# The last 32 rows of each expert, handled in two groups of four experts

## What is computed

```
mask1 = one_hot(argmax(softmax(tokens @ gate_w + gate_b)), 8)
pos   = number of earlier tokens of the same expert;  keep = pos < 160
dispatch = einsum('nec,nd->ecd', mask1 x one_hot(pos) x keep, tokens)
h          = gelu(dispatch @ w1 + b1)        # 8 experts, 160 x 256 -> 160 x 1024
expert_out = h @ w2 + b2                     # 160 x 1024 -> 160 x 256
out = x + gate probability x expert_out, put back at the token's row
```

## Time and profile before

| | us |
|---|---|
| median of three runs (1109.96 to 1110.98) | 1110.84 |
| the profiled execution's own time | 1106.06 |
| its span in the profile | 1104.1 |
| expert stage, first transpose to the last matmul of L778 | 1013.1 to 1094.1 |
| from there to the end of the span | 10.0 |

### The profile page before, as it was taken

The page is one execution under the profiler, slowest core; times in us unless marked ns, Lnnn a source line. Parts: engine busy times, 40 slices in busy tenths (PEclk is TensorE's granted clock), DMA queues, the critical chain, the costliest instruction groups (busy, mean ns, idle before and its releaser), DMA issues.

```text
span 1104.1 us, 40835 instructions
## 1 busy us (share of the span) xinstructions
PE 1066.6 (97%) x16195; PEld 869.6 (79%) x16195; DVE 882.3 (80%) x2652; ACT 796.4 (72%) x2319; POOL 244.1 (22%) x521
## 2 busy tenths in 40 slices
PE   6899999999999999999999999999999999988996
PEld 5678787787888788887787888788888778766996
DVE  6788798898888888888898888888888888874211
ACT  5778687788787787787787787787787787742221
POOL 1011212222222222212222222222222222221112
PEclk9999999999999999999999999999999999999998
DMA  7333422222221222112222221222212221001673
GB/s 202 109 101 102 154 63 67 68 68 64 60 64 44 61 62 57 49 50 60 61 61 61 60 60 42 59 56 56 48 48 58 58 61 36 17 12 47 207 249 110
DMA packets 69260, 82.04 MB, mean 74 GB/s; under 512 B 14331, under 2 KB 48076, under 8 KB 69072
## 3 DMA queue, kind: packets, MB, share of 16 engines
q1 hardware_dynamic: 64896, 75.06, 23.6%
q0 software_dynamic: 3360, 3.72, 1.0%
q10 hardware_dynamic: 816, 0.66, 0.2%
HBM read 64.79 MB, written 16.56 MB: 74 GB/s over the span
## 4 chain that ended last, share of the span: by engine, by line
PE 72%; DVE 18%; issue 4%; DMA 2%; ACT 1%; SPq 1%; POOL 1%; POOLq 0%; DVEq 0%; ACTq 0%
PE kps L416 12%; PE vps L428 12%; PE score L462 9%; PE score L448 5%; PE gather L477 5%; PE shared L486 5%; PE shared L501 4%; DVE prob L1092 4%; DVE nmx L1081 4%; PE score L778 3%; PE score L764 3%; PE shared L527 3%; DVE ctx_p L1073 2%; PE shared L405 2%; DVE th L1175 2%
## 5 line engine op out<-in xcount | busy, mean ns | idle before, releaser
L830 ACT ACTIVATE prob<-score,nmx 128x257 f32<-128x257 f32 x512 | 235.8, 475 | 95.8 <-DVE nmx L1081 95.8
L416 PE MATMUL kps<-ctx_p,wk_p 128*128 128x512 f32 x768 | 217.4, 411 | 0.0
L428 PE MATMUL vps<-wv_p,ctx_p 128*128 128x256 f32 x1536 | 215.5, 290 | 0.0
L1081 DVE TENSOR_REDUCE nmx<-score 128x2 f32<-128x514 f32 x256 | 165.2, 687 | 59.2 <-PE score L448 59.0
L428 PEld LDWEIGHTS vps<-wv_p,ctx_p 128*128 128x128 f32 x1536 | 191.7, 190 | 14.1 <-issue 12.7
L416 PEld LDWEIGHTS kps<-ctx_p,wk_p 128*128 128x128 f32 x768 | 138.1, 190 | 38.5 <-issue 13.6
L1092 DVE TENSOR_SCALAR prob<-prob,rsum 128x256 f32<-128x256 f32 x512 | 159.3, 354 | 9.1
L462 PE MATMUL score<-const,prob 128*128 128x128 f32 x1024 | 153.5, 278 | 5.5 <-DVE prob L1092 3.3
L1558 POOL TENSOR_TENSOR rstd<-ve,const 128x1 f32<-128x1 f32 x64 | 53.2, 831 | 464.6 <-DVE ve L1210 235.7
L462 PEld LDWEIGHTS score<-const,prob 128*128 128x128 f32 x1024 | 114.7, 141 | 16.3 <-DVE prob L1092 14.9
L847 ACT ACTIVATE ctx_p<-ctxT,nlast 128x256 fp32r<-128x256 f32 x256 | 116.0, 511 | 4.2 <-issue 4.2
(11 more groups left out here) (227 smaller groups left out, 1734.7 us busy)
## 6 DMA issues: line engine op xcount, KB each, us to landing
ctxT<-in_ctxT SPq DMA_DIRECT2D x128, 257.0 KB, 3.2
w<-in_w SPq DMA_DIRECT2D x16, 1024.0 KB, 8.1
xq<-in_x SPq DMA_DIRECT2D x32, 128.0 KB, 2.1
xr<-in_x SPq DMA_DIRECT2D x32, 128.0 KB
qbd<-qkT SPq DMA_DIRECT2D x248, 16.0 KB, 1.8
out<-row SPq DMA_DIRECT2D x31, 128.0 KB
slots<-row SPq DMA_DIRECT2D x10, 257.0 KB, 5.1
x_a<-slots SPq DMA_DIRECT2D x8, 129.0 KB, 2.1
```

Of the source, the lines that this page charges most:

```text
L416: last = mm(kps[:, :], wk_p[:, x, n, c * P:(c + 1) * P], ctx_p[:, y, n, 2 * r:2 * r + 2, :].rearrange("p j s -> p (j s)"), start=(n, x) == ...
L428: last = mm(vps[:, c, :], ctx_p[:, x, n, j, c * P:(c + 1) * P], wv_p[:, y, n, :], start=(n, x) == (0, LO), stop=(n, y) == (C - 1, LO))
L830: last = af(prob[:, m, :], score[:, m, 0:S], ACT.Exp, bias=nmx[:, m:m + 1], scale=1.0, accum_out=esum[:, m:m + 1])
L1081: v.tensor_reduce(nmx[:, 2 * c:2 * c + 2], score[:, 2 * c:2 * c + 2, 0:S], AX.X, ALU.max, negate=True).then_inc(s["max_done"], 1)
```

## The change

The 128-row part stays as it was. The 32-row parts of experts 0 to 3 share one tile of 128 partitions, and those of experts 4 to 7 another: they are loaded with four DMAs into 32 partitions each, transposed together, and copied with two instructions to the columns 128 to 159 of a `disp` that now has a place for every expert. The second bias is added in two instructions for the 128 columns and two for the 32 columns, the latter into `eo_rest`, which collects four experts; after experts 3 and 7 that tile is transposed, added (`fb`, 128 rows) and written with one indirect DMA. Loads of the first group are issued half by SyncE and half by ScalarE. The declarations of the new semaphores and unchanged lines are left out here.

```diff
--- before.py
+++ after.py
@@ -25,6 +25,7 @@
 CR = CAP - P
+GROUP = P // CR
 ROW = 2 * D + 2
@@ -167,14 +168,15 @@
-        y_a, y_b = sb("y_a", [P, 2, D]), sb("y_b", [CR, 2, D])
-        x_a, x_b = sb("x_a", [P, 2, ROW - D]), sb("x_b", [CR, 2, ROW - D])
+        y_a, y_b = sb("y_a", [P, 2, D]), sb("y_b", [P, 2, D])
+        x_a, x_b = sb("x_a", [P, 2, ROW - D]), sb("x_b", [P, 2, ROW - D])
         gelu_table = sb("gelu_table", [P, 1])
         table = sb("table", [P, 2])
-        disp = sb("disp", [P, C, CAP])
+        disp = sb("disp", [P, E, C, CAP])
         hid = sb("hid", [P, FT, CAP])
-        eo = sb("eo", [P, C, CAP])
-        fa, fb = sb("fa", [P, 2, D]), sb("fb", [CR, 2, D])
+        eo, eo_rest = sb("eo", [P, C, P]), sb("eo_rest", [P, C, P])
+        fa, fb = sb("fa", [P, 2, D]), sb("fb", [P, 2, D])
@@ -348,20 +351,28 @@
-            def load_rows(e, r, a_, b_, columns, done):
-                sp.dma_start(a_[:, r, :], slots[bass.ds(CAP * e, P), columns]).then_inc(s[f"{done}{r}"], 16)
-                sp.dma_start(b_[:, r, :], slots[bass.ds(CAP * e + P, CR), columns]).then_inc(s[f"{done}{r}"], 16)
+            def load_rows(e, r, dst, columns, done):
+                sp.dma_start(dst[:, r, :], slots[bass.ds(CAP * e, P), columns]).then_inc(s[f"{done}{r}"], 16)
+            def load_rest(g, dst, columns, done, members=range(GROUP)):
+                for m in members:
+                    e = GROUP * g + m
+                    sp.dma_start(dst[CR * m:CR * (m + 1), g, :], slots[CAP * e + P:CAP * (e + 1), columns]).then_inc(s[f"{done}{g}"], 16)
+            load_rows(0, 0, y_a, slice(0, D), "y_in")
+            load_rest(0, y_b, slice(0, D), "y_rest", range(1, GROUP, 2))
+            load_rows(1, 1, y_a, slice(0, D), "y_in")
             for r in range(2):
-                load_rows(r, r, y_a, y_b, slice(0, D), "y_in")
-            for r in range(2):
-                load_rows(r, r, x_a, x_b, slice(D, ROW), "x_in")
+                load_rows(r, r, x_a, slice(D, ROW), "x_in")
+            load_rest(1, y_b, slice(0, D), "y_rest")
+            for g in range(2):
+                load_rest(g, x_b, slice(D, ROW), "x_rest")
             for i in range(0, E // 2 - 1):
 ...
                     sp.wait_ge(s["dt_ps"], e + 1)
-                    load_rows(e + 2, r, y_a, y_b, slice(0, D), "y_in")
+                    load_rows(e + 2, r, y_a, slice(0, D), "y_in")
@@ -372,10 +383,11 @@
-                    sp.wait_ge(s[f"fin_out{r}"], 32 * i + 32)
-                    load_rows(e + 2, r, x_a, x_b, slice(D, ROW), "x_in")
+                    sp.wait_ge(s[f"fin_out{r}"], 16 * i + 16)
+                    load_rows(e + 2, r, x_a, slice(D, ROW), "x_in")
             for r in range(2):
-                sp.wait_ge(s[f"fin_out{r}"], 32 * (E // 2))
+                sp.wait_ge(s[f"fin_out{r}"], 16 * (E // 2))
+            sp.wait_ge(s["rest_out"], 32)
             sp.wait_ge(s["x2_out"], 16 * T)
@@ -725,20 +737,25 @@
             hps = [score[:, m, 0:3 * CAP].rearrange("p (f n) -> p f n", f=3) for m in range(3)]
-            dps = shared[:, 0:C * CAP].rearrange("p (c n) -> p c n", c=C)
+            dps, rps = sh_c, gather[:, :, 0, :]
             ops_ = score[:, 3, 0:C * CAP].rearrange("p (c n) -> p c n", c=C)
 ...
                 e = 2 * i + r
-                pe.wait_ge(s[f"y_in{r}"], 32 * (i + 1))
+                pe.wait_ge(s[f"y_in{r}"], 16 * (i + 1))
                 pe.wait_ge(s["dt_evac"], e)
                 for c in range(C):
-                    nc.tensor.transpose(dps[:, c, 0:P], y_a[:, r, c * P:(c + 1) * P], k["ident"])
-                    last = nc.tensor.transpose(dps[:, c, P:CAP], y_b[:, r, c * P:(c + 1) * P],
-                                               k["ident"][0:CR, 0:CR])
+                    last = nc.tensor.transpose(dps[:, c], y_a[:, r, c * P:(c + 1) * P], k["ident"])
                 last.then_inc(s["dt_ps"], 1)
+            def transpose_rest(g):
+                pe.wait_ge(s[f"y_rest{g}"], 16 * GROUP)
+                for c in range(C):
+                    last = nc.tensor.transpose(rps[:, c], y_b[:, g, c * P:(c + 1) * P], k["ident"])
+                last.then_inc(s["rest_ps"], 1)
@@ -747,21 +764,26 @@
                 for c in range(C):
-                    nc.tensor.transpose(kps[:, c * P:(c + 1) * P], eo[:, c, 0:P], k["ident"])
-                    last = nc.tensor.transpose(vps[0:CR, 0, c * P:(c + 1) * P], eo[:, c, P:CAP], k["ident"])
+                    last = nc.tensor.transpose(kps[:, c * P:(c + 1) * P], eo[:, c, :], k["ident"])
                 last.then_inc(s["et_ps"], 1)
+                if e % GROUP == GROUP - 1:
+                    pe.wait_ge(s["eo_rest"], e + 1)
+                    for c in range(C):
+                        last = nc.tensor.transpose(vps[:, 0, c * P:(c + 1) * P], eo_rest[:, c, :], k["ident"])
+                    last.then_inc(s["et_rest"], 1)
 ...
                 pe.wait_ge(s["dt_evac"], e + 1)
+                pe.wait_ge(s["rest_done"], e // GROUP + 1)
                 pe.wait_ge(s[f"w1_in{r}"], 16 * (i + 1))
 ...
                     for c in range(C):
-                        last = mm(hps[f // 3][:, f % 3, :], w1[:, r, c, f * P:(f + 1) * P], disp[:, c, :],
+                        last = mm(hps[f // 3][:, f % 3, :], w1[:, r, c, f * P:(f + 1) * P], disp[:, e, c, :],
                                   start=c == 0, stop=c == C - 1)
@@ -769,8 +791,10 @@
                     transpose_dispatched(i + (r + 1) // 2, (r + 1) % 2)
+                if once(e, 1):
+                    transpose_rest(1)
                 pe.wait_ge(s[f"w2_in{r}"], 16 * (i + 1))
-                pe.wait_ge(s["eo_done"], e)
+                pe.wait_ge(s["eo_rest"], e)
                 for c in range(C):
@@ -780,6 +804,7 @@
             transpose_dispatched(0, 0)
+            transpose_rest(0)
             expert(0, 0, before=False)
@@ -1013,6 +1038,10 @@
             af(gelu_table[:, :], k["ones"][:, 0:1], ACT.Gelu_apprx_tanh)
+            act.wait_ge(s["sent"], 16 * T)
+            for m in range(0, GROUP, 2):
+                act.dma_start(y_b[CR * m:CR * (m + 1), 0, :], slots[CAP * m + P:CAP * (m + 1), 0:D]).then_inc(s["y_rest0"], 16)
             act.wait_ge(s["ffb_done"], 1)
@@ -1508,37 +1537,54 @@
-            dps = shared[:, 0:C * CAP]
             ops_ = score[:, 3, 0:C * CAP].rearrange("p (c n) -> p c n", c=C)
 ...
                 dve.wait_ge(s["dt_ps"], e + 1)
-                dve.wait_ge(s["h_ps"], floor0(3 * e))
-                v.tensor_copy(disp[:, :, :].rearrange("p c n -> p (c n)"), dps).then_inc(s["dt_evac"], 1)
+                v.tensor_copy(disp[:, e, :, 0:P], sh_c).then_inc(s["dt_evac"], 1)
+            def rest_dispatched(g):
+                dve.wait_ge(s["rest_ps"], g + 1)
+                for c in range(C):
+                    last = v.tensor_copy(disp[:, GROUP * g:GROUP * (g + 1), c, P:CAP],
+                                         gather[:, c, 0, :].rearrange("p (m n) -> p m n", m=GROUP))
+                last.then_inc(s["rest_done"], 1)
 ...
                 e = 2 * i + r
+                g = e // GROUP
                 if after:
                     dispatched(e + 1)
+                if once(e, 1):
+                    rest_dispatched(1)
                 dve.wait_ge(s["eo_ps"], e + 1)
                 dve.wait_ge(s["et_ps"], e)
-                for c in range(C):
-                    last = v.tensor_scalar(eo[:, c, :], ops_[:, c, :], b2_of(e, c), None, ALU.add)
+                dve.wait_ge(s["et_rest"], g)
+                for c in range(C):
+                    last = v.tensor_scalar(eo[:, c, :], ops_[:, c, 0:P], b2_of(e, c), None, ALU.add)
                 last.then_inc(s["eo_done"], 1)
+                m = e % GROUP
+                for c in range(C):
+                    last = v.tensor_scalar(eo_rest[:, c, CR * m:CR * (m + 1)], ops_[:, c, P:CAP], b2_of(e, c), None, ALU.add)
+                last.then_inc(s["eo_rest"], 1)
                 dve.wait_ge(s["et_ps"], e + 1)
-                dve.wait_ge(s[f"x_in{r}"], 32 * (i + 1))
-                dve.wait_ge(s[f"fin_out{r}"], 32 * i)
+                dve.wait_ge(s[f"x_in{r}"], 16 * (i + 1))
+                dve.wait_ge(s[f"fin_out{r}"], 16 * i)
                 v.scalar_tensor_tensor(fa[:, r, :], kps[:, 0:D], x_a[:, r, D:D + 1], x_a[:, r, 0:D],
-                                       ALU.mult, ALU.add)
-                v.scalar_tensor_tensor(fb[:, r, :], vps[0:CR, 0, :], x_b[:, r, D:D + 1], x_b[:, r, 0:D],
                                        ALU.mult, ALU.add).then_inc(s["fin_done"], 1)
+                if e % GROUP == GROUP - 1:
+                    dve.wait_ge(s["et_rest"], g + 1)
+                    dve.wait_ge(s[f"x_rest{g}"], 16 * GROUP)
+                    v.scalar_tensor_tensor(fb[:, g, :], vps[:, 0, :], x_b[:, g, D:D + 1], x_b[:, g, 0:D],
+                                           ALU.mult, ALU.add).then_inc(s["rest_fin"], 1)
 ...
             dispatched(0)
+            rest_dispatched(0)
```

(21 more changed lines are left out.)

## The result

| | before | changed |
|---|---|---|
| median | 1109.93 us (6 runs, 1107.41 to 1110.98) | 1102.62 us (6 runs, 1099.25 to 1104.02) |
| profiled execution, its span | 1106.06, 1104.1 | 1104.02, 1102.2 |
| end of the first L764 (L786) block to the last matmul | 74.82 | 68.74 |
| last matmul to the end of the span | 10.0 | 8.9 |

The ratio is 0.9934 with an interval of 0.992 to 0.9948: 7.3 us faster, between 5.8 and 8.9.

What follows compares the result with a forecast made beforehand. TensorE, busy for 97% of the span, was taken as the bound. Terms -3.4 - 1.3 - 0.14 - 1.5 + 0.4 + 0.1 - 0.2 were summed to -6.1: 1106.06 to 1099.9, plus 4.78 gives 1104.7 us, range 1103.3 to 1107.3.

Steps and rivals of the forecast that it cites:

- the tail: After the last matmul: shorter bias additions, earlier release of scatters, last scatter with 128 rows; -0.2 us, between -0.5 and +0.3.
- the base: Profiled execution's 1106.06 us plus the 4.78 by which the median lay higher, a distance kept for the forecast.
- The stream: TensorE's work in the expert stage: terms -3.4, -1.3, -0.14, -1.5 and +0.4 us.
- the row transposes: Experts 1 to 7 on TensorE: two wide transposes at 0.22 us replace four at 0.71; 3.4 us saved, at least 2.4.
- the product: Second product behind the row transposes: 4.36 instead of 4.54 us in seven experts; 1.3 us saved, between 0 and 1.3.
- the late rows: Expert 7's first row transpose, waiting for its load: 0.25 us falls to 0.11, saving 0.14.
- the result transposes: Inside the first product: two of four at 0.11 us go in seven experts; 1.5 us saved.
- two added pairs: Transposes added in experts 1 and 4 for the second group's rows and first group's results; +0.4 us, at most 1.0.
- the price of a wide pair: Two 128 x 128 row transposes in a row on TensorE: 0.11 us each, or from the other side 0.11 and 0.26.
- Rival A: SyncE's loop of scatter, issues and weights becomes the bound in late experts; 1106.4 us at 10 us a turn; chance 10%.
- the start: Before expert 0's first product: the group's four loads, transposes and copies cost +0.1 us, between 0 and +0.7.
- Rival C: First group lands 2 us late, TensorE idles and expert 0's products run at half clock; 10.7 us lost, 1115.4; chance 4%.

Runs made afterwards that it cites:

- e1: Kernel before with each expert's row transposes ordered wide, wide, narrow, narrow; 73.8 us from first product's first block to last matmul, against 74.8.
- e2: Kernel before with each expert's row transposes ordered narrow, narrow, wide, wide; 73.3 us from first product's first block to last matmul, against 74.8.
- e3: Kernel before with only the rows' loads and transposes grouped by four experts, results per expert as before; 1105.60 us, ratio 0.9973 to the kernel before.
- e6: Kernel before with each expert's 32-row scatter issued ahead of its 128-row one; 75.3 us from first product's first block to last matmul, against 74.8.
- e5: Changed kernel with three held matmuls before and three behind the group's row transposes at the start; 1101.33 us, ratio 0.9923 to the kernel before.
- e4: Kernel before with only the results grouped by four experts, rows loaded and transposed per expert; 1104.83 us, ratio 0.9965 to the kernel before.
- e7: Changed kernel with two more 32-row loads per expert in SyncE's queue, into an unread tile; 68.73 us from first product's first block to last matmul.
- e9: Changed kernel with the first group's scatter issued again after experts 3, 4, 5 and 6; GpSimd's closing drain 4.24 us, against 3.92.
- e10: e2 with SyncE's residual-row loads moved behind the next expert's y, w1 and w2; 72.52 us from first product's first block to last matmul, against 73.3.

## Why the prediction was right or wrong

The time came out below the stated range, and two steps of the prediction put it there: the tail, a term of -0.2 that measured -1.1, and the base, 1110.84, some 1 to 1.5 us above where more runs put the kernel before. Had either been right, the range moved with it would have held the time. The stream, nine tenths of the change, was right in mechanism and size.

**Right: the stream.** The sum had 3.4 + 1.3 + 0.14 + 1.5 - 0.4 = 5.94 us for it and 6.08 was measured; 0.1 of the difference is rounding of the 0.11 steps. Each term holds by itself: the row transposes 0.71 to 0.22, the product 4.54 to 4.35, the late rows' 0.14 gone, the result transposes 0.44 to 0.22, two added pairs of 0.22. An expert's window is 9.13 or 9.14, as announced, and a fifth of a microsecond more where an added pair stands. Where the text had to choose between ends (the price of a wide pair, the 0.18 of the product), the nearest rows gave the right one, and e1 and e2 show the reason that was argued.

**Right, for part of the reason: the DMA.** Rival A (10%) did not come, but its loop is real. It stalls by 0.64 to 0.94 us in e1, e2 and e3, where only TensorE's side gets quicker, and by 0.14 in the kernel before and 0.6 in e6. The prediction gave the change 1.7 us of lead at expert 7. `y_a` had 4.29 where 2.5 are needed, 1.8 over, and this agreement is luck: the slow first product had added to it. With that product at full clock e5 had 3.38, 0.9 over. The prediction named both reasons, the issues (0.9 us) and the wait; the issues were worth at most 0.3, so the wait weighs more.

**Wrong: the tail.** Forecast -0.2 (-0.5 to +0.3), measured -1.1. The failed step of this term is "It carries 128 rows instead of 32: 0.97 instead of 0.88, and some 0.3 more to land." It took the last landing for what sets the end. GpSimd's drain sets it, and it ends 2.6 to 3.3 us later, its length counted in scatters: six fewer, 0.49 us. The start of the last scatter, thought to come 0.1 to 0.6 sooner, came 0.66 sooner: the first scatter is released by `fa` at 1.65 us after the last matmul instead of by `fb` at 2.31, as the prediction said, and the second kept its distance of 1.28, so all of this gain reached the end.

**Too small, within its bounds: the start.** +0.1 forecast within 0 to +0.7; 3.86 us on average from the first load to the first product with the old rows and 4.21 with grouped ones (without e5 and its added matmuls), so +0.35. A small load was taken at 1.9 us at most, and the last of four landed after 2.31. The clock at half for part of the first product, at times, was not foreseen. Rival C had that mechanism, with a price of 10.7 us and a single long gap; it came at some 1.6 us, in two profiles of five. Its "decides from a delay of about 2 us on" was not what the runs show.

**Wrong: the base.** The sum was put on a median of three runs, and the failed step is "I keep that distance: 1104.7 us." The stage's terms as measured, -6.1 - 1.1 + 0.35, give -6.8, and with the slow first product now and then some -6.2, inside the measured 5.8 to 8.9. Against 1110.84, where the prediction started, that would be 1104.0 and still in the range. The median of three runs was 0.9 us above that of six (1109.93) and 1.5 above that of 23 (1109.36), and the low end of the range was made from "the upper bounds with 0.7 of scatter between medians". Single runs of one kernel spread over 5 to 7 us here (1099.25 to 1104.02; 1105.05 to 1111.95), and two medians of few runs can each be off by 1. In hindsight, with 0.9 more for the tail and 1 more for the base, the range would have begun near 1101.5.

**Wrong: some of the adding up.** The terms of the sum give -6.0, not -6.1. Their bounds added up give -2.0 to -6.4, not "-3.0 to -6.8", so the low end of the range was already 0.4 us lower than its own terms allow, and the high end too low. Neither decides anything here.

**Open.** SyncE's first load of the stage goes out on average 2.0 us later in the six profiles with grouped rows (1014.2) than in the six others (1012.2), though nothing before it was changed. The medians show no such loss, since the whole change gained as much as its stage or more. Part of it goes with the granted clock of the first part: up to that load it averages 0.995 in the kernel before, e2, e4, e7, e9 and e10, which get there at 1010.7 to 1013.6, and 0.988 to 0.993 in the six others, which get there at 1012.3 to 1015.2. Whether the rest, and the clock itself, is chance was not tried.

## What to carry to other kernels

When an engine is busy throughout a stage, price an instruction by the distance between starts in the chain, and compare the same instruction in its different neighbourhoods: here some three quarters of the 0.68 us that the 32-row transposes cost were the changes of shape around them, and reordering alone returned more than a third of it. Before speeding up the busy engine, look how far ahead its loads are asked for, and take waits for outputs out of the queue that feeds it. Before comparing how far ahead a load is in two kernels, see that nothing earlier, such as a slow first product, has moved one of them. Ask what ends the span: here it was not the last landing. For small gains, read the stage from marks inside it, and take the base and its spread from many runs.

## What the hardware showed that was not expected

- A change between 128-row and 32-row transposes costs TensorE about 0.13 us, as the mean of the two directions (e1, e2), while 32 columns beside 128 cost nothing beyond the 0.11 step.
- GpSimd's closing drain ends 0.08 us later after the last scatter instruction for each indirect DMA of the program (3.92, 4.24 and 4.41 us for 42, 46 and 48). The ones that were added or left out all lie in the expert stage, in e9 in the middle of it.
- A scatter that takes 2.0 us alone lands after 6.76 while weights are moved (e2), and holds up a queue that waits for it, although the same bytes in another order of that queue pass without a stall (e10).
